# A two-layer scan, FFN and mixture-of-experts kernel on one core: scan in halves, product with C and small norm steps on GpSimd, FFN normalisation on ScalarE, new order tables

## What is computed

```python
x = x + 0.5 * L0_ffn(layernorm(x))      # "ffn1": layernorm, 128->512 (ternary weights), gelu, layernorm, 512->128
x = x + L0_attn(layernorm(x))           # a 16-state scan along the positions, times gelu(z), 128->128
x = x + 0.5 * L0_ffn(layernorm(x))      # "ffn2"
x = x + 0.5 * L1_ffn(x)                 # "moef": encode, route to 2 of 8 experts, decode, layernorm
x = x + L1_attn(x)                      # selective scan, below
x = x + 0.5 * L1_ffn(x)                 # "moeb"
```

```python
dA  = exp(delta[l, d] * A[d, n])
dBu = delta[l, d] * u[l, d] * B[l, n]
state = dA * state + dBu
y[l, d] = sum_n state[l, d, n] * C[l, n]
```

## Time and profile before

| | us |
|---|---|
| median of 3 runs | 1466.05 |
| lowest and highest of them | 1443.38, 1468.54 |
| the profiled execution | 1452.7 |
| its span, first to last instruction | 1451.0 |
| DVE busy in it | 1000.1 |
| PE busy | 1144.1 |
| ACT busy | 680.0 |
| POOL busy | 601.7 |

### The profile page before, as it was taken

How to read it: one execution, slowest core, us unless ns; L and a number is a source line. 1 busy time by engine, 2 the same in 40 slices (tenths; PEclk the granted TensorE clock), 3 DMA queues, 4 the chain that set the end, 5 groups by cost and what they waited for, 6 DMA issues and landing times.

```text
span 1451.0 us, 12541 instructions
## 1 busy us (share of the span) xinstructions
PE 1144.1 (79%) x4326; PEld 666.5 (46%) x4326; DVE 1000.1 (69%) x1607; ACT 680.0 (47%) x1034; POOL 601.7 (41%) x314
## 2 busy tenths in 40 slices
PE   0647889879989897888798798889678776866866
PEld 0425655645547354554445363545335342432425
DVE  2232435377766788877977857899779899698722
ACT  1132445464645545847382555655643624633330
POOL 0012121264543547544553535554655746365210
PEclk9957578777977888979997798979869789797865
DMA  3000000133340335323323323343345445356100
GB/s 92 1 7 8 1 0 8 54 130 116 123 140 29 124 106 162 119 94 116 116 97 123 116 66 118 117 145 117 125 145 174 147 155 175 115 173 210 58 7 8
DMA packets 50840, 142.80 MB, mean 98 GB/s; under 512 B 6741, under 2 KB 17241, under 8 KB 50777
## 3 DMA queue, kind: packets, MB, share of 16 engines
q1 hardware_dynamic: 50776, 142.01, 29.8%
HBM read 139.37 MB, written 2.62 MB: 98 GB/s over the span
## 4 chain that ended last, share of the span: by engine, by line
PE 39%; DVE 34%; ACT 12%; issue 7%; POOL 5%; DMA 2%; SPq 1%; POOLq 0%; DVEq 0%; ACTq 0%
DVE hs L858 14%; PE mp L1200 7%; PE yp L1299 6%; DVE hs L861 5%; PE mp L1191 5%; PE fp L1116 3%; PE fp L1130 3%; ACT he L974 3%; PE fp L1124 2%; POOL dbu L563 2%; ACT L883 2%; DMA bcast<-held 2%; ACT dA L1068 2%; DVE eo L780 2%; DVE f_z L651 2%
## 5 line engine op out<-in xcount | busy, mean ns | idle before, releaser
L563 POOL TENSOR_TENSOR dbu<-du,bcast 128x1024 f32<-128x1024 f32 x128 | 372.3, 2912 | 334.3 <-DVE hs L858 224.3
L1299 PE MATMUL yp<-hs,ident 128*128 128x512 f32 x512 | 300.0, 718 | 75.6 <-DVE hs L861 75.4
L858 DVE TENSOR_TENSOR_SCAN hs<-dA,dbu 128x1024 f32<-128x1024 f32 x128 | 292.5, 2285 | 51.4 <-PE yp L1299 34.7
L1068 ACT ACTIVATE dA<-delta,mA 128x496 f32<-128x496 f32 x256 | 162.9, 669 | 202.7 <-DVE hs L858 201.9
L1299 PEld LDWEIGHTS yp<-hs,ident 128*128 128x128 f32 x512 | 105.7, 223 | 219.5 <-DVE hs L861 112.3
L861 DVE TENSOR_TENSOR hs<-hs,bcast 128x1024 f32<-128x1024 f32 x128 | 175.6, 1372 | 4.4
L1200 PE MATMUL mp<-w_e,he 128*128 128x64 f32 x1024 | 153.8, 323 | 13.7 <-ACT he L974 11.9
L1200 PEld LDWEIGHTS mp<-w_e,he 128*128 128x128 f32 x1024 | 152.3, 238 | 26.5 <-ACT he L974 17.1
L1191 PE MATMUL mp<-cont,w_e 64*128 64x512 f32 x256 | 123.6, 836 | 34.9 <-DVE lg L737 25.1
L974 ACT ACTIVATE he<-mp,vectors 128x512 f32<-128x512 f32 x128 | 82.3, 682 | 90.4 <-PE mp L1191 89.9
L883 ACT ACT_TABLE_LOAD x75 | 96.2, 1283 | 1.3
(11 more groups left out here) (204 smaller groups left out, 1653.3 us busy)
## 6 DMA issues: line engine op xcount, KB each, us to landing
bcast<-held SPq DMA_DIRECT2D x128, 1024.0 KB, 5.4
xin<-L_attn_x SPq DMA_DIRECT2D x8, 256.0 KB, 2.9
out<-xo SPq DMA_DIRECT2D x8, 256.0 KB, 3.0
held<-bc SPq DMA_DIRECT2D x8, 64.0 KB, 2.6
he<-conv_wT SPq DMA_DIRECT2D x1, 384.0 KB
w<-w1T SPq DMA_DIRECT2D x1, 256.0 KB
he<-w2T SPq DMA_DIRECT2D x1, 256.0 KB
w_e<-L_ffn_W SPq DMA_DIRECT2D x2, 128.0 KB
```

What stands on the lines that cost most here:

```text
L563: pool.tensor_tensor(out=dbu[:, j % 2, :].rearrange("p (r t) -> p r t", r=2), in0=d, in1=b_n, op=ALU.mult).then_inc(dbu_r.sem, 1)
L858: dve.tensor_tensor_scan(out=h, data0=dA[:, :], data1=dbu[:, j % 2, :], initial=0.0, op0=ALU.mult, op1=ALU.add).then_inc(hs_r.sem, 1)
L1068: ins = act.activation(out=dst, in_=src, func=ACT.Exp, scale=mA[:, c, 2 * k + r:2 * k + r + 1])
L1299: last = pe.matmul(yp[:, :], lhsT=ident[:, :], rhs=hs[:, j % 2, r * SEQ:(r + 1) * SEQ], start=(k == 0 and r == 0), stop=(k == PAIRS - 1 an ...
```

## The change

1. The scan of a step is split in two instructions of 512 columns, one for each state and bank of `dA`. ACT's exponential of a half waits for the scan two halves back, where it waited for the whole step before.
2. The product with C moves from DVE to POOL, as a thread of its own (`Y`). `hs` gets a third buffer (`HELD`).
3. Of every norm, the step `vv` (DVE before) and the shift `nb` go to POOL, which now issues four small instructions for each norm in place of one. ACT waits for POOL alone. The last small step of the FFN's second norm (`fvar`, maximum and product) goes to POOL too.
4. F's normalisation (`f_z`, 96 instructions of 128x128) goes from DVE to ACT.
5. The sum into `hx` and `xo` that ends a MoE turn goes from DVE to POOL; the semaphore `m_done` is gone. POOL's sums `f_xp`, `m_xp`, `p_xp` get a letter of their own and now wait until the normalisation of the same x is done.
6. All tables of `ORDER` are new (one line is shown here).

```diff
     "DVE":
-        "FFFFFFFFFFFFFFMFMFFFMFMFFMFFMFMMFFFMFMMMPMPFFFFMMFFFFMFMMMPFFFMFMMMMPPPSFSFFSFMMSSFFSSMFMFMFMSPSSSMM"
+        "FFFFFFFFFFFMFMMFFMMMMFFFFMPFFFMPFFFPSSSMMFFFSFMMSSSMSMSSSSSFSFFSSMMSSSPSSFFFSSSSPMMFSFSFSMMMMPFSSMSS"
...
 SLOTS = 3
+HELD = 3
...
-            def rstd(src, dst, var, done, turn):
-                pool.wait_ge(var.sem, var.at(turn, 1))
-                pool.tensor_tensor(out=dst, in0=src, in1=neg_half[:, :], op=ALU.pow).then_inc(done.sem, 1)
+            def rstd(norm, turn, double=False):
+
+                by, plus = (1.0 + EPS, EPS * EPS) if double else (1.0, EPS)
+                pool.wait_ge(norm.var.sem, norm.var.at(turn, 1))
+                ch.add(pool.tensor_scalar(out=norm.vv[:, :], in0=norm.mv[:, :, 1], scalar1=by, scalar2=plus,
+                                          op0=ALU.mult, op1=ALU.add))
+                ch.add(pool.tensor_scalar(out=norm.nb[:, :], in0=norm.mv[:, :, 0], scalar1=-1.0, scalar2=None,
+                                          op0=ALU.mult))
+                ch.wait()
+                ch.add(pool.tensor_tensor(out=norm.rs[:, :], in0=norm.vv[:, :], in1=neg_half[:, :], op=ALU.pow))
+                ch.wait()
+                pool.tensor_tensor(out=norm.nb[:, :], in0=norm.nb[:, :], in1=norm.rs[:, :],
+                                   op=ALU.mult).then_inc(norm.rstd.sem, 1)
...
+                    pool.wait_ge(ddg.sem, ddg.at(m, 1))
+                    pool.tensor_tensor(out=dst[:, :, :], in0=mxp[:, m % 2, :, :], in1=dd[:, :, :],
+                                       op=ALU.add).then_inc(done.sem, 1)
...
+            def y_thread():
+                for j in range(BATCH * STEPS):
+                    yield True
+                    pool.wait_ge(hs_r.sem, 2 * (j + 1))
+                    h = hs[:, j % HELD, :]
+                    pool.tensor_tensor(out=h, in0=h, in1=bcast[:, j % SLOTS, 1, :], op=ALU.mult).then_inc(hc_r.sem, 1)
...
-                            dve.wait_ge(dA_r.sem, j + 1)
-                            dve.wait_ge(dbu_r.sem, j + 1)
-                            if j >= 2:
-                                dve.wait_ge(sum_ps.sem, j - 1)
-                            h = hs[:, j % 2, :]
-                            dve.tensor_tensor_scan(out=h, data0=dA[:, :], data1=dbu[:, j % 2, :], initial=0.0,
-                                                   op0=ALU.mult, op1=ALU.add).then_inc(hs_r.sem, 1)
-                            dve.wait_ge(hs_r.sem, j + 1)
-                            dve.tensor_tensor(out=h, in0=h, in1=bcast[:, j % SLOTS, 1, :],
-                                              op=ALU.mult).then_inc(hc_r.sem, 1)
+                            for r in range(2):
+                                yield True
+                                dve.wait_ge(dA_r.sem, 2 * j + r + 1)
+                                if r == 0:
+                                    dve.wait_ge(dbu_r.sem, j + 1)
+                                    if j >= HELD:
+                                        dve.wait_ge(sum_ps.sem, j - HELD + 1)
+                                half = slice(r * SEQ, (r + 1) * SEQ)
+                                dve.tensor_tensor_scan(out=hs[:, j % HELD, half], data0=dA[:, half],
+                                                       data1=dbu[:, j % 2, half], initial=0.0,
+                                                       op0=ALU.mult, op1=ALU.add).then_inc(hs_r.sem, 1)
...
             def ffn(stage, i, f, l):
                 yield True
+                normed(fn, 3 * i + l, fz, fx if f else xin, fzn)
+                yield True
                 turned(fzT[:, :], fps[0], fzt_ps, fzt, 3 * i + l)
```

More of the change, by code:

```diff
@@ L52 @@
-    "ACT":
[L53 to L58, removed]
@@ L488, in ffn @@
                 yield True
[L489 to L493, removed]
-                else:
-                    pool.wait_ge(x2.sem, x2.at(i, 1))
+                rstd(fn, 3 * i + l, True)
+                yield True
+                pool.wait_ge(fzn.sem, (3 * i + l + 1) * TILES)
                 pre_add(fxp[:, :, :], x, bias2, fxpre)
                 yield True
-                rstd(fvar[:, :], frs[:, :], fv, fr, 2 * i + f)
+                pool.wait_ge(fv.sem, fv.at(2 * i + f, 1))
+                ch.add(pool.tensor_scalar(out=fvar[:, :], in0=fvar[:, :], scalar1=EPS, scalar2=4.0,
+                                          op0=ALU.max, op1=ALU.mult))
+                ch.wait()
+                pool.tensor_tensor(out=frs[:, :], in0=fvar[:, :], in1=neg_half[:, :], op=ALU.pow).then_inc(fr.sem, 1)
             def f_thread():
@@ L635, in stats @@
                 for q in range(TILES):
-                    ch.add(dve.bn_aggr(out=norm.mv[:, q, :], in_=norm.st[:, q, :]))
-                ch.wait()
-                by, plus = (1.0 + EPS, EPS * EPS) if double else (1.0, EPS)
-                dve.tensor_scalar(out=norm.vv[:, :], in0=norm.mv[:, :, 1], scalar1=by, scalar2=plus,
-                                  op0=ALU.mult, op1=ALU.add).then_inc(norm.var.sem, 1)
-            def shift(norm, turn):
-                dve.wait_ge(norm.rstd.sem, norm.rstd.at(turn, 1))
-                dve.scalar_tensor_tensor(out=norm.nb[:, :], in0=norm.mv[:, :, 0], scalar=-1.0, in1=norm.rs[:, :],
-                                         op0=ALU.mult, op1=ALU.mult).then_inc(norm.nbr.sem, 1)
-            def normed(x, turn):
-                dve.wait_ge(fn.rstd.sem, fn.rstd.at(turn, 1))
-                for q in range(TILES):
-                    dve.tensor_scalar(out=fz[:, q, :], in0=x[:, q, :], scalar1=fn.mv[:, q, 0:1],
-                                      scalar2=fn.rs[:, q:q + 1], op0=ALU.subtract,
-                                      op1=ALU.mult).then_inc(fzn.sem, 1)
+                    ins = dve.bn_aggr(out=norm.mv[:, q, :], in_=norm.st[:, q, :])
+                    if q < TILES - 1:
+                        ch.add(ins)
+                    else:
+                        ins.then_inc(norm.var.sem, 1)
             def update(dst, src, scale, l, i, done):
@@ L681, in ffn @@
                 ch.wait()
[L682 to L686 removed]
+                dve.scalar_tensor_tensor(out=fvar[:, :], in0=o[:, :, P + 1], scalar=EPS, in1=fvar[:, :],
+                                         op0=ALU.add, op1=ALU.subtract).then_inc(fv.sem, 1)
                 yield True
@@ L895, in normed @@
             def normed(norm, turn, dst, src, done):
-                act.wait_ge(norm.nbr.sem, norm.nbr.at(turn, 1))
+                act.wait_ge(norm.rstd.sem, norm.rstd.at(turn, 1))
                 for q in range(TILES):
```

153 lines of the change are left out of this document (68 added, 85 removed).

## The result

| | before | after |
|---|---|---|
| median, us | 1461.98 (4 runs, 1443.38 to 1468.54) | 1348.97 (4 runs, 1341.68 to 1353.17) |
| profiled execution and its span | 1452.7, 1451.0 | 1348.6, 1346.7 |

The ratio is 0.929 (95%: 0.919 to 0.940). Some executions of one and the same kernel take longer at a lower granted clock, and every ratio here leaves these out, so that it is not quite the quotient of the medians shown. Against the forecast of 1335 us the median is 14 us longer. The total came out as forecast, but the reason given for it did not hold, as the experiments show. The granted clock is a little higher after the change (0.836 in the profiled execution, 0.816 before). That is not the gain: a run of the kernel before at 0.835 took 1431.6 us, 83 more than the 1348.6 at 0.836.

What follows compares the result with a forecast made beforehand. The prediction took DVE, 86% busy in a fixed order, as the bound, with PE close behind. Its stretches summed to 1324 us, 1326 with time outside the span, times 1.009 1338, stated as 1335 us; range 1240 to 1430.

Steps and rivals of the forecast that it cites:

- A DVE that is 86% busy with an order fixed beforehand makes M's small DVE steps wait; that is the bound I see.: Kernel before, stretch from 1052 us: DVE busy 276 of 321 us delays M's small steps, PE close behind in the middle.
- The turn table: Whole span, stretch by stretch over the 16 MoE turns with their scan steps: 1451 us before, 1324 us forecast.
- The factor of 1.009: Conversion of the profiled execution into a median, 1466.05 / 1452.7: 1326 us becomes 1338 us.
- the 65 us of a light turn: Turns with 5 to 9 scan steps: 64 us of the last turn, plus waits behind POOL, less the clock's gain.
- A gain of 2 to 3 us a turn, no more: Between two turns, the chain from `dd` to the next `m_z` loses one pair of statistics and the DVE sum.
- Turn 2, 107 us: Dense turn with 14 scan steps: 109 us before, forecast at 107 us.
- POOL's waits for `bcast` above 109 us: Sign in the changed profile: slots held longer by the product on POOL; POOL waited 109 us in 48 waits before.
- The 0.3 us of signals: In the scan loop, signalling time added to the 5.4 us DMA that refills a freed `bcast` slot.
- Per-engine sums: Forecast busy time of each engine after the change: DVE 691, POOL 901, ACT 739 us; PE unchanged.
- the dear-steps rival: Small POOL norm steps cost 1.06 us each, POOL rises to 1070 us: median 1535 us; chance 0.09.
- The rival of POOL's queue: POOL at 68% delays M's four visits per turn, light turns take 72 us: about 1400; 0.23 with the other 1400 case.
- The new order is not what the time goes by: PE and its clock set turns 2 to 10, only 11 to 15 shrink: about 1400; 0.23 with the other 1400 case.

Runs made afterwards that it cites:

- experiment 2: Kernel before, old tables, with half scans, three `hs` buffers and the product with C on GpSimd: 1468.1 us, ratio 1.026.
- experiment 4: Kernel before with only the small variance and shift steps of all norms moved to GpSimd: 1457.4 us, ratio 1.013.
- experiment 5: Kernel before with small norm steps and `hx`/`xo` sum on GpSimd, next turn's statistics right behind those of `dd` in 9 turns: 1454.1 us, ratio 1.015.
- experiment 10: Old tables with all work given out as in the changed kernel, only product and FFN normalisation letters set in anew: 1477 us, ratio 1.024.
- experiment 9: Changed kernel's tables with product, sums, small steps and FFN normalisation back on VectorE; half scans and third buffer kept: 1370 us, ratio 0.946.
- experiment 1: Changed kernel with the product with C back on VectorE, all else as changed: 1342.1 us, ratio 0.936.
- Experiment 6: Changed kernel in which the statistics of 11 turns wait on VectorE for the previous turn's sum: 1368.6 us, ratio 0.959.
- experiment 8: Changed kernel with an added GpSimd power of 4 columns behind each of the 128 products with C: 1430.8 us, ratio 1.001.
- experiment 11: Kernel before with 256 added VectorE reductions of 512 columns, two together behind each product with C: 1503.4 us, ratio 1.042.

## Why the prediction came out, and what in it was wrong

- *"A DVE that is 86% busy with an order fixed beforehand makes M's small DVE steps wait; that is the bound I see."* This step failed, as far as it takes DVE's load for the bound: the fixed order mattered, and not how full DVE was. The new tables with a DVE 983 us busy gained 85 us, and in turns 3 to 10 a DVE that was 85% busy served shorter turns. Four versions with a relieved DVE on the old tables (experiments 2, 4, 5 and 10) gained nothing, and load added to the old DVE cost 0.53 to 0.67 of its busy time.
- *The turn table* was nearly right, 1324 for 1347 us. It used the number of steps in each turn, which is a matter of the tables, and apart from turn 2 its errors, up to 14 us in a stretch, cancelled. That the total came out although the reason for the short turns was wrong is in good part luck. The factor of 1.009 from the profiled execution to the median was not borne out either (1348.6 and 1349.0 us); it made up for 12 of the 23 us that were missing. I explained the 65 us of a light turn by DVE being free; experiment 9 has the same length for turns 11 to 14 without that.
- *"A gain of 2 to 3 us a turn, no more"* for the border: it was 8.4 us in turns 3 to 14. I costed the instructions on the chain from `dd` to `m_z`, and not the queue ahead of each. I had both orders before me and didn't count the letters between.
- *Turn 2, 107 us:* it took 130. The border behind it is 55 us, since turn 3 waits for F. I counted its steps and forgot that M's next input comes from a thread that the same dense steps slow down.
- *POOL's waits for `bcast` above 109 us:* 9.3 us. I took the held slots as a cost of the loop. The 0.3 us of signals in it were too much too: the trace of the kernel before has 0.07 us from the product's end to the next issue and 0.07 from the landing to `dbu`. POOL releases them itself now and is the busier engine, so the DMA has mostly landed when POOL comes to it. The runs agree, whatever the tables: the wait is 18.1 and 20.2 us in experiments 2 and 10, with the product on POOL, and 65.5 and 72.3 us in experiments 1 and 9, with it on DVE.
- *Per-engine sums:* POOL 901 forecast, 894.7 measured; ACT 739 and 732.5; DVE 691 and 712.7. Small steps on POOL 0.25 forecast, 0.19 to 0.24 measured, so the dear-steps rival fell.
- *The rival of POOL's queue* was right in kind: POOL has 31% of the chain, and 1.05 us more for each step costs 82 us or more. It hadn't set in at 66% busy with this row: with the product off POOL (experiment 1) the time is the same.
- *"The new order is not what the time goes by"* was the reverse of what the runs show.

What stays open: which part of the new tables does it. The short borders (101 us in turns 3 to 14) and the 16 steps moved out of the last four turns overlap: of the 91 us of these turns 31 lie in borders and 60 inside the turns. No run changed the places of the steps alone. Experiment 6 shows that the border is on the path, for 20 to 43 us of it. PE, 91% busy in turns 5 to 9, is the nearest to a bound there, and no run made it lighter. What a lighter DVE is worth by itself is open too, since every version that relieves it loads GpSimd in its place, and experiment 8 shows that such load can cost. That could hide a gain in experiments 2 and 10; experiments 9 and 11 don't depend on it. In experiments 9 and 10 the added letters were placed by a model and not tuned, so the 22 us lost in 10 may be a matter of these letters. That they also hide a gain of 100 us seems unlikely, but no run shows it.

## What to carry to other kernels

Where queues are fixed in order, count what stands ahead of each short step of the longest chain in the new order, and how many long pieces fall into each of its stretches; busy shares of 70 to 86% said little about the bound here. When a change moves work and rewrites the order, try the two apart in both directions before giving the gain to either. And a price measured by adding load (0.67 to 0.85 us for each us here) need not hold for load taken away (nothing here).

## What the runs showed of the hardware

- Small GpSimd instructions of 4 columns are cheap: 0.19 us for a `tensor_scalar` on `m_vv`, 0.23 for `m_nb`, 0.20 for the product with the power, against 1.03 us for the power itself.
- GpSimd's product of 128x1024 with two SBUF inputs takes 2.35 us in the middle, 2.80 at most, beside half scans on VectorE, and these take 1.21 us, 1.23 at most: the scans are not delayed at all and the products hardly. With the product on VectorE (experiment 1) `dbu` has a mean of 2.72 us and the product one of 1.51. The Trainium skill (SBUF — State Buffer, "Who interferes with whom") has an exclusive lock on the ports that the two share; these rows agree.
- The Trainium skill (GPSIMD Engine Reference, "Engine selection") gives two-input elementwise work to VectorE. By the instruction that holds (2.36 us against 1.51 here), but the kernel takes 1342 us with the product on VectorE and 1349 with it on GpSimd: in this kernel the placement of the product decides nothing.
